# A gated cross-attention and quantised feed-forward kernel on one Trainium2 core: the first feed-forward pass is cut into chunks of 1024 columns in place of pieces of 512

## What is computed

```
def act_qdq(x):                       # one scale for the whole tensor
    scale = jnp.maximum(jnp.max(jnp.abs(x)) / 32767, 1e-12)
    return jnp.clip(jnp.round(x / scale), -32768, 32767) * scale

x    = x + tanh(g_xattn) * cross_attention(layernorm(x), ctx)
h    = act_qdq(layernorm(x))
up   = act_qdq(h @ w_up.T)            # weights quantised in blocks of 32
gate = act_qdq(h @ w_gate.T)
sig  = round_to_u16(sigmoid(gate))    # steps of 1/65536
gate = act_qdq(gate * sig)
o    = act_qdq(gate * up)
out  = x + tanh(g_ffn) * (o @ w_down.T)
```

## Time and profile before

| | us |
|---|---|
| median of 3 runs | 563.86 (563.69 to 564.0) |
| the profiled execution, its own time | 564.34 |
| its span in the profile | 562.2 |
| mean granted TensorE clock of it | 0.976 of full speed |

### The profile page before, as it was taken

How to read it: one execution, slowest core, us unless ns; L and a number is a source line. 1 busy time by engine, 2 the same in 40 slices (tenths; PEclk the granted TensorE clock), 3 DMA queues, 4 the chain that set the end, 5 groups by cost and what they waited for, 6 DMA issues and landing times. The chain is left out here.

```text
span 562.2 us, 10767 instructions
## 1 busy us (share of the span) xinstructions
PE 515.2 (92%) x3936; PEld 457.9 (81%) x3936; DVE 407.4 (72%) x915; ACT 311.7 (55%) x960; POOL 139.6 (25%) x149
## 2 busy tenths in 40 slices
PE   3899999999999999999999999999789999608898
PEld 3877988988998998899899899887667878505897
DVE  3667877666656755765576676878776879999896
ACT  2663543554354264346335436455378569988992
POOL 3010421231121123123113113124123029920000
PEclk9899999999999999999999999999999999958899
DMA  7942000200110110011011001005001000100033
GB/s 229 375 147 77 1 1 1 89 8 1 56 37 0 56 37 0 0 64 29 0 56 37 0 1 39 1 2 170 1 19 39 0 1 0 39 0 1 1 113 112
DMA packets 18493, 25.85 MB, mean 46 GB/s; under 512 B 1232, under 2 KB 15824, under 8 KB 18464
## 3 DMA queue, kind: packets, MB, share of 16 engines
q1 hardware_dynamic: 18208, 25.17, 13.3%
q0 software_dynamic: 256, 0.30, 0.4%
HBM read 21.27 MB, written 4.19 MB: 45 GB/s over the span
## 5 line engine op out<-in xcount | busy, mean ns | idle before, releaser
L1665 POOL TENSOR_TENSOR probs<-probs,rinv 128x512 f32<-128x512 f32 x64 | 66.4, 1043 | 229.0 <-DVE rinv L1226 229.0
L883 ACT ACTIVATE probs<-bank,nmax 128x128 f32<-128x128 f32 x256 | 90.8, 380 | 25.0 <-DVE nmax L1218 25.0
L628 PE MATMUL bank<-wv,ctxT 128*128 128x512 f32 x384 | 94.0, 399 | 1.9 <-DVE v L1145 1.9
L620 PE MATMUL bank<-ctxT,wk 128*128 128x256 f32 x672 | 89.1, 282 | 0.3 <-DVE ctxT L1104 0.3
L628 PEld LDWEIGHTS bank<-wv,ctxT 128*128 128x128 f32 x384 | 70.9, 188 | 20.6 <-DVE v L1145 2.6
L620 PEld LDWEIGHTS bank<-ctxT,wk 128*128 128x128 f32 x672 | 83.6, 188 | 0.5 <-DVE ctxT L1104 0.5
L853 ACT ACTIVATE qk<-bank 128x256 f32<-128x256 f32 (+1 forms) x60 | 24.0, 400 | 94.6 <-PE bank L620 92.9
L1230 DVE COPY pT<-bank 128x512 f32<-128x512 f32 x64 | 41.1, 684 | 42.1 <-PE bank L687 42.0
L883 ACT ACTIVATION_READ_ACCUMULATOR probs<-bank,nmax 128x1 f32 x256 | 56.6, 221 | 0.0
L620 PE MATMUL bank<-xnT,wq 128*128 128x256 f32 x336 | 51.9, 290 | 0.1
L660 PE MATMUL bank<-wout,oT 128*128 128x256 f32 x384 | 47.3, 282 | 1.7 <-DVE oT L1235 0.9
(11 more groups left out here) (167 smaller groups left out, 920.9 us busy)
## 6 DMA issues: line engine op xcount, KB each, us to landing
craw<-in_ctx SPq DMA_DIRECT2D x8, 512.0 KB, 3.6
stage<-in_L_xattn_Wkv SPq DMA_DIRECT2D x8, 512.0 KB, 12.3
xa<-in_x SPq DMA_DIRECT2D x8, 256.0 KB, 2.7
xr<-in_x SPq DMA_DIRECT2D x8, 256.0 KB, 2.9
x_scratch<-y SPq DMA_DIRECT2D x7, 256.0 KB, 2.2
x2all<-x_scratch SPq DMA_DIRECT2D x1, 1536.0 KB, 7.0
xres<-x_scratch SPq DMA_DIRECT2D x6, 256.0 KB, 2.9
out<-yout SPq DMA_DIRECT2D x6, 256.0 KB, 2.2
```

The source lines that it names most:

```text
L620: last = mm(bk[:, n * TG:(n + 1) * TG], wt[a][:, k, f], act_t[b][:, k, :], start=(k == 0 and i == 0), stop=(k == kk - 1 and i == len(TERMS ...
L628: last = mm(bk[:, :], ctxT[a][:, k, b * S:(b + 1) * S], wv[w][:, k, h * 512:(h + 1) * 512], start=(k == 0 and i == 0), stop=(k == KC - 1 a ...
L883: nc.scalar.activation(probs[:, p % 2, h, u, :], score_bank[p % 2][h][:, u * S:(u + 1) * S], ACT.Exp, bias=nmax[:, p % 2, h, u:u + 1], acc ...
L1665: G.tensor_tensor(probs[:, p % 2, h, :, :], probs[:, p % 2, h, :, :], rinv[:, p % 2, h, :].rearrange("p (u o) -> p u o", o=1).to_broadcast ...
```

## The change

- The 24 pieces become 14 chunks (`CHUNKS`): pieces 0 and 1 alone, ten chunks of two neighbouring pieces (1024 columns: two feature tiles of the same 512 tokens), pieces 22 and 23 alone. All loops of the first pass on ScalarE, VectorE and POOL now run over chunks.
- The rings keep their slot counts (`tgi` and `tsi` 6, `tsg` 4) with slots twice as wide. To find room `tsi` lies where the gate and up weights begin (the gate weights are read for the last time before the pass), and `tsg` reaches over the places of `tpi`, `yout` and `xres`. The float copy of x that used `tsg` has a name of its own (`xf`).
- Because `tsg` covers `xres`, the first two residual loads on SP wait for `p_ready` = `NCK + 1`, which is the end of the pass. The load of `xlast` stands behind them.
- `by_vector` is now chunks 4, 8 and 13, `gate_by_scalar` chunks 1, 4, 7 and 10. POOL rounds the gate three chunks ahead in place of four pieces.
- `up_maximum` covers two pieces (1024 columns): two of them stand before the first product, in place of five of 512.
- ScalarE evicts `up` pieces in ones and twos between the sigmoids (`ups_needed`).

```diff
@@ -237,6 +237,9 @@
         NCH = KI * B * S // CH
         HC = CH // 2
         GS = 6
+        CHUNKS = [(0, 1), (1, 1)] + [(n, 2) for n in range(2, 4 * KI - 2, 2)] + [(4 * KI - 2, 1), (4 * KI - 1, 1)]
+        NCK = len(CHUNKS)
         OR = 8
         stack[0] = ffn
@@ -244,6 +247,10 @@
         stack[0] = early
         wg = [sb(f"wg{i}", [P, KD, I], F32R) for i in range(2)]
         wu = [sb(f"wu{i}", [P, KD, I], F32R) for i in range(2)]
+        early.close()
+        early = ExitStack()
+        stack[0] = early
+        tsi = sb("tsi", [P, GS, CH], U16)
         early.close()
         stack[0] = ffn
         oI = [sb("oI0", [P, 2, KI, 512], F32R)]
@@ -270,12 +277,15 @@
         stack[0] = ffn
         xT = [sb(f"xT{i}", [P, KD, B * S], F32R) for i in range(2)]
         gate = sb("gate", [P, KI, B * S])
-        tgi = sb("tgi", [P, GS, HC], I16)
-        tsi = sb("tsi", [P, GS, HC], U16)
+        tgi = sb("tgi", [P, GS, CH], I16)
         tui = sb("tui", [P, 4, CH], I16)
         early = ExitStack()
         stack[0] = early
-        tsg = sb("tsg", [P, 4, HC])
+        tsg = sb("tsg", [P, 4, CH])
+        early.close()
+        early = ExitStack()
+        stack[0] = early
+        xf = sb("xf", [P, 4, KD * TG])
         early.close()
         stack[0] = ffn
         tpi = sb("tpi", [P, 4, CH], I16)
@@ -410,19 +420,37 @@
         def xfloat(t):
-            return tsg[:, t % 4, :].rearrange("p (k s) -> p k s", k=KD)
+            return xf[:, t % 4, :].rearrange("p (k s) -> p k s", k=KD)
         def gate_piece(n):
             return gate[:, n % KI, n // KI * HC:(n // KI + 1) * HC]
-        def by_vector(q):
-            return q % 6 == 5
-        def gate_by_scalar(q):
-            return q % 3 == 1
+        def gate_chunk(c):
+            n, w = CHUNKS[c]
+            j, columns = n % KI, slice(n // KI * HC, (n // KI + 1) * HC)
+            return gate[:, j, columns] if w == 1 else gate[:, j:j + 2, columns]
+        def width(c):
+            return CHUNKS[c][1] * HC if c < NCK else 1
+        def like_gate(ring, c):
+            if width(c) < CH:
+                return ring[:, c % GS, 0:width(c)]
+            return ring[:, c % GS, :].rearrange("p (j s) -> p j s", j=2)
+        def ups_needed(c):
+            return min(4 * KI, sum(CHUNKS[c]) + 4) if c >= 0 else 4
+        def by_vector(c):
+            return c in (4, 8, NCK - 1)
+        def gate_by_scalar(c):
+            return c in (1, 4, 7, 10)
         def gate_made(engine, q):
             if gate_by_scalar(q):
@@ -548,6 +576,7 @@
             def load_residual(t):
                 sp.dma_start(xres[:, t % 2, :, :], x2_t[:, 2 * t:2 * t + 2, :]).then_inc(xres_ld[t % 2], 16)
+            sp.wait_ge(p_ready, NCK + 1)
             load_residual(0)
             load_residual(1)
             sp.wait_ge(gu_out, 8 * KI)
@@ -1022,32 +1051,32 @@
             up_c = up[:, :, :].rearrange("p j t -> p (j t)")
             act.wait_ge(x2_out, 16 * NG)
-            def sigmoid(q):
-                n = HC if q < 4 * KI else 1
-                gate_made(act, q)
-                if q >= 4 and by_vector(q - 4):
-                    act.wait_ge(p_ready, q - 3)
-                elif q >= 4:
-                    act.wait_ge(si_ready, pool_made(q - 4))
-                nc.scalar.activation(tsg[:, q % 4, 0:n], tgi[:, q % GS, 0:n], ACT.Sigmoid,
+            def sigmoid(c):
+                gate_made(act, c)
+                if c >= 4 and by_vector(c - 4):
+                    act.wait_ge(p_ready, c - 3)
+                elif c >= 4:
+                    act.wait_ge(si_ready, pool_made(c - 4))
+                nc.scalar.activation(tsg[:, c % 4, 0:width(c)], tgi[:, c % GS, 0:width(c)], ACT.Sigmoid,
                                      scale=small[:, 10:11]).then_inc(sg_ready, 1)
-            def gate_integers(q):
-                if q >= GS:
-                    act.wait_ge(p_ready, q - GS + 1)
-                nc.scalar.activation(tgi[:, q % GS, :], gate_piece(q), act_copy,
+            def gate_integers(c):
+                if c >= GS:
+                    act.wait_ge(p_ready, c - GS + 1)
+                nc.scalar.activation(like_gate(tgi, c), gate_chunk(c), act_copy,
                                      scale=small[:, 11:12]).then_inc(gi_scalar, 1)
-            for q in range(4):
-                gu(1, q)
+            for n in range(4):
+                gu(1, n)
             act.wait_ge(scale_ready, 1)
             gate_integers(1)
-            for q in range(4 * KI + 1):
-                if q + 2 < 4 * KI and gate_by_scalar(q + 2):
-                    gate_integers(q + 2)
-                sigmoid(q)
-                if q + 4 < 4 * KI:
-                    gu(1, q + 4)
+            for c in range(NCK + 1):
+                if c + 2 < NCK and gate_by_scalar(c + 2):
+                    gate_integers(c + 2)
+                sigmoid(c)
+                if c < NCK:
+                    for n in range(ups_needed(c - 1), ups_needed(c)):
+                        gu(1, n)
             act.wait_ge(scale_ready, 2)
@@ -1480,8 +1509,8 @@
             def up_maximum(n):
                 tg, j = n // KI, n % KI
-                dve.wait_ge(gu_out, 4 * KI + n + 1)
-                return V.tensor_reduce(amax[:, 1, n:n + 1], up[:, j, tg * 512:(tg + 1) * 512], AX.X, ALU.max,
+                dve.wait_ge(gu_out, 4 * KI + n + 2)
+                return V.tensor_reduce(amax[:, 1, n:n + 2], up[:, j:j + 2, tg * 512:(tg + 1) * 512], AX.X, ALU.max,
                                        apply_absolute_value=True)
             def scale_column(src):
@@ -1514,31 +1543,30 @@
-            ahead = 5
-            for q in range(ahead):
-                up_maximum(q).then_inc(gu_max, 1)
-            for q in range(4 * KI):
-                if by_vector(q):
-                    dve.wait_ge(sg_ready, q + 1)
-                    link(V.tensor_scalar(tsi[:, q % GS, :], tsg[:, q % 4, :], 65536.0, None, ALU.mult))
+            for n in range(0, 4, 2):
+                up_maximum(n).then_inc(gu_max, 1)
+            for c in range(NCK):
+                if by_vector(c):
+                    dve.wait_ge(sg_ready, c + 1)
+                    link(V.tensor_scalar(tsi[:, c % GS, 0:width(c)], tsg[:, c % 4, 0:width(c)], 65536.0, None, ALU.mult))
                 else:
-                    dve.wait_ge(si_ready, pool_made(q))
-                V.tensor_tensor_reduce(gate_piece(q), tgi[:, q % GS, :], tsi[:, q % GS, :], -1.0, 0.0,
-                                       ALU.mult, ALU.max, amax[:, 2, q:q + 1]).then_inc(p_ready, 1)
-                if q + ahead < 4 * KI:
-                    up_maximum(q + ahead).then_inc(gu_max, 1)
-                if q == 4 * KI - ahead:
-                    dve.wait_ge(gu_max, 4 * KI)
+                    dve.wait_ge(si_ready, pool_made(c))
+                V.tensor_tensor_reduce(gate_chunk(c), like_gate(tgi, c), like_gate(tsi, c), -1.0, 0.0,
+                                       ALU.mult, ALU.max, amax[:, 2, c:c + 1]).then_inc(p_ready, 1)
+                if ups_needed(c) % 2 == 0 and ups_needed(c) > ups_needed(c - 1):
+                    up_maximum(ups_needed(c) - 2).then_inc(gu_max, 1)
+                if ups_needed(c) == 4 * KI > ups_needed(c - 1):
+                    dve.wait_ge(gu_max, 2 * KI)
                     scale_column(amax[:, 1, 0:4 * KI])
-                if q == 4 * KI - ahead + 1:
+                if c and ups_needed(c - 1) == 4 * KI > ups_needed(c - 2):
                     scale_values(2, s1(7), 13, 12, s1(4))
-            dve.wait_ge(si_ready, pool_made(4 * KI))
-            V.tensor_tensor(amax[:, 2, 4 * KI:4 * KI + 1], tgi[:, 4 * KI % GS, 0:1], tsi[:, 4 * KI % GS, 0:1],
+            dve.wait_ge(si_ready, pool_made(NCK))
+            V.tensor_tensor(amax[:, 2, NCK:NCK + 1], tgi[:, NCK % GS, 0:1], tsi[:, NCK % GS, 0:1],
                             ALU.mult).then_inc(p_ready, 1)
-            dve.wait_ge(p_ready, 4 * KI + 1)
-            scale_column(amax[:, 2, 0:4 * KI + 1])
+            dve.wait_ge(p_ready, NCK + 1)
+            scale_column(amax[:, 2, 0:NCK + 1])
             scale_of_row(3, 15, s1(8))
             link(V.reciprocal(s1(3), s1(15)))
             V.tensor_scalar(s1(16), s1(3), s1(14), None, ALU.mult)
@@ -1715,29 +1743,25 @@
             up_c = up[:, :, :].rearrange("p j t -> p (j t)")
             pool.wait_ge(scale_ready, 1)
-            def gate_integers(q):
-                if q >= GS:
-                    pool.wait_ge(p_ready, q - GS + 1)
-                n, src = (HC, gate_piece(q)) if q < 4 * KI else (1, small[:, 6:7])
-                G.tensor_scalar(tgi[:, q % GS, 0:n], src, small[:, 11:12], 1.0, ALU.mult,
-                                ALU.mult).then_inc(gi_ready, 1)
-            def sigmoid_integers(q):
-                n = HC if q < 4 * KI else 1
-                pool.wait_ge(sg_ready, q + 1)
-                G.tensor_scalar(tsi[:, q % GS, 0:n], tsg[:, q % 4, 0:n], 65536.0, 1.0, ALU.mult,
+            def gate_integers(c):
```

(29 more changed lines are left out.)

## The result

| | before | changed |
|---|---|---|
| median of 12 runs, us | 563.92 | 565.02 |
| range of the runs, us | 562.84 to 566.78 | 564.01 to 565.83 |
| ratio to before, 95% interval | | 1.0019 (1.001 to 1.0027) |
| profiled execution, its own time, us | 564.34 | 565.83 |
| its span, us | 562.2 | 563.7 |

The changed kernel is slower by 1.1 us, 0.19%. The interval lies above 1, so the sign is that of the forecast; the size is far from the forecast 2.6 us.

A forecast was written before the change was run, and what follows sets the result against it. VectorE products and POOL roundings excluding each other bound the first pass; 27.5 us of work from 465.5, plus 5.6 of waits, less 0.2, ends it at 498.4; ScalarE's chain makes the shift +2.6 us: 566.5 us, range 563.2 to 568.2.

The forecast's parts named there:

- The sign: Whole kernel: slower, given 0.70, against 0.17 for within 0.2% and 0.13 for faster.
- what it does to the waits: First pass from 465.5: 27.5 us of VectorE work plus 5.6 us of waits behind POOL roundings, ending at 498.4.
- six, 5.6 us: First pass: six waits behind POOL roundings of 1024, 5.6 us; bounds were five, 4.7 us, and eight, 7.4 us.
- The price: One wait of a product behind a POOL rounding of 1024: 0.39 plus 0.54, 0.93 us.
- the correction of 0.2: 0.2 us off the waits, because two of the catches fall on a VectorE rounding, shorter than a product.
- The work: VectorE's remaining work in the first pass from 465.5: 31.0 less 3.5, 27.5 us, 493.0 with no wait.
- The second way to the same number: Shared resource taken by POOL and VectorE until 491.6, then VectorE alone 6.3 to 7.5 us: pass ends 497.9 to 499.1.
- The opening: Start of first pass: POOL's wide chunk 3 gate rounding delays the second product to end at 465.5; about 1.5 us lost.
- The gain: VectorE's first pass: wider instructions cut its work from 32.1 to 31.0 us, a gain of 1.1 us.
- The wait does not grow with the width: Rival, faster: each wait stays 0.39 us, five cost 2.0 in place of 5.6; 562.9 us; faster given 0.13.
- VectorE wins the near ties: Rival, no change: VectorE first two times in three, three long waits left, 2.8 us; 563.7 us; no change given 0.17.
- What was named to look for: Products of 1.2 and about 2.1 us, five to seven long; VectorE alone some 6 us; ScalarE idle before its roundings.

The follow-up runs named there:

- e6: The changed kernel with POOL's first-pass roundings left out, POOL writing constants of the same shape and reading no SBUF: 562.37 us, one execution.
- e7: The kernel before with POOL's first-pass roundings left out, POOL writing constants of the same shape and reading nothing: 561.31 us, one execution.
- e2: The changed kernel with each POOL rounding of 1024 columns issued as two of 512: 566.05 us, ratio to before 1.0052.
- e4: The changed kernel with the last pair maximum of `up` before chunk 10's product and the scale of `up` right behind that product: 564.38 us, ratio to before 1.0015.
- e5: The kernel before with only the rings in the new homes with wide slots and the residual loads behind the pass: 563.57 us, ratio 1.0.
- e3: The changed kernel with POOL rounding the second sigmoid before the gate of chunk 3: 564.86 us, ratio to before 1.0025.
- e9: The changed kernel rearranged: no sigmoid roundings on VectorE, other short chunks and ScalarE gates, POOL four chunks ahead, mixed maxima: 560.89 us, ratio to before 0.995.

## Why the prediction was right or wrong

**The sign** held, and so did parts of the mechanism. A product and a POOL rounding exclude each other (e6, e7), a wide rounding makes a longer wait (e2), and ScalarE's chain over the scale of `up` decides the start of the second pass (e4), which is 0.69 of the 1.24 us. The residual loads and the homes cost nothing (e5), and the shift went through to the end but for 0.2 us. **What did not hold is that longer waits lengthen the pass.** In the forecast the time that VectorE is held grows from 3.5 to 5.4 us; it stayed at 3.5. That the pass grew all the same, by 0.55 us, came from idle time. So the right sign is in part luck.

**The size** was +1.1 in place of +2.6 us. The step that failed is "what it does to the waits". Measured from the first maximum, I had the second product end at 7.1 (465.5 - 458.41), and it ended at 7.05. The pass was to be over at 40.0, and was at 38.6. The term between is "six, 5.6 us":

- *The price.* I took 0.93 us for a wait behind a long rounding, by adding to 0.39 the 0.54 us that 512 more columns cost VectorE. They cost POOL 0.43: a sigmoid rounding of 1024 in the changed kernel lasts 1.04 us where one of 512 lasted 0.61. The measured wait is 0.79 to 0.80. Six times 0.14 is 0.8 us.
- *The count.* Three products were caught for the full 0.8 us (at 475.64, 478.72 and 481.80), two for 0.36 us and a rounding of VectorE's own for 0.39; 0.8 us more was idle time before the product of chunk 3. Together 4.3 us, 3.5 of them held. I had written 5.4 after the correction of 0.2.
- *The work.* The rest of it was 27.2 us in place of 27.5: a long sigmoid rounding takes 0.72 to the next start and a maximum 1.13.

From the scale of `up` the chain ran as costed: scale to second pass 5.48 us against 5.6, with 0.80 us of idle time on VectorE where I had 0.7. Carried through with the measured end of the pass it gives the measured start.

**The second way to the same number was false comfort.** It took the shared resource as full until 491.6. It wasn't: POOL waited 4.7 us for sigmoids. ScalarE, which now took its `up` pieces in twos, stood 2.5 us longer for TensorE than before, and two wide sigmoids went to VectorE and not to POOL; how the 4.7 us divide between the two was not tested. Two sums that share an assumption don't check each other. ScalarE was late for POOL, not for VectorE: after the opening VectorE's only idle time, 0.80 us at 470.36, ended on a rounding of POOL that stood behind another which the product of chunk 2 had held (2.18 us from 467.13).

**The opening** was right in its times and wrong in its cause: e3 took the delay of the second product away, and the same idle time stood before the third. Which of the wide steps on ScalarE and POOL brings the opening's extra idle time was not run one by one.

**The gain** from wider instructions was there as work (some 1.3 us against the 1.1 of the sum), but not as time: 1.8 us more of idle time ate it. Where no product is held, 0.24 us of it was left in the pass (e6 against e7), with the two reservations made there.

**The rivals.** "The wait does not grow with the width" is refuted by the products of 2.0 us. "VectorE wins the near ties" was partly so: the product of chunk 2, 0.06 us behind POOL, went first, and the one at 475.64, 0.17 us behind, did not. The case of no change was given 0.17, with a price of 563.7; what came, 565.02, lies at the very lower end of the forecast, 565.0, and its mechanism is nearer to this rival's "only three long waits are left". The range of 563.2 to 568.2 takes it in, but it was drawn wide enough for two mechanisms.

**What was named to look for**: products in two lengths, found (1.2 and 2.0, with two at 1.6), but three of the long kind and not five to seven; VectorE alone at its products for some 6 us at the end, found, but 4.4 us (POOL through at 34.2, the pass over at 38.6); ScalarE idle before its roundings, found, 4.04 us.

## What to carry to other kernels

Where two engines exclude each other, count the waits at the width of the other engine's instruction and with the other engine's own cost per column, and then ask which engine has idle time after the change: the chunks made room on POOL, and the gain came with arrangements that moved VectorE's roundings into it and made the scale of `up` earlier (3 us in all, e9). An edit that delays an instruction in the opening costs nothing if the next one waits for something else; remove the delay in an experiment before charging for it. An engine's own saving per instruction (some 1.3 us here) is not a saving of time while others set its pace. And split a pass into own work, time held and idle time before and after the change: here that alone shows that the held time, which the forecast was about, did not grow.

## What the runs showed of the hardware

- Who goes first in a near tie is not settled by the start alone. A product that started 0.05 to 0.07 us behind a gate rounding on POOL went ahead of it (472.57 before; 467.19 and 470.36 in the changed kernel), and one 0.09 or 0.17 us behind a POOL rounding was held (473.78 before; 475.64 in the changed kernel). But the product at 467.79 of the kernel before, 0.06 us behind the rounding of a sigmoid, was held too (1.09 us).
- POOL instructions that only write never held a product back: none of the 14 products of e6 and the 24 of e7 is stretched. They did hold a rounding on VectorE with one tensor to read: 0.83 us in place of 0.41, three times in e7, each beside a constant that POOL began to write 0.03 us later. A maximum was held in no run.
- 512 more columns cost POOL 0.43 us in a rounding and VectorE 0.53 to 0.54 us in a maximum or a product (0.28 in a rounding), so a wait for POOL grows less with width than the instruction that waits.
